# Evicting the output projection of a linear-attention layer from PSUM in two halves

## What is computed

```python
def ffn(x, weight):                       # binarised weights
    return jnp.einsum('bsi,oi->bso', x, jnp.sign(weight))
def attn(x, ...):                         # linear attention, 16 heads of 64
    Q = phi(x @ Wq.T + bq); K = phi(x @ Wk.T + bk); V = x @ Wv.T + bv   # phi = elu + 1
    KV = jnp.einsum('bhnd,bhne->bhde', K, V)
    out = jnp.einsum('bhnd,bhde->bhne', Q, KV)
    norm = jnp.einsum('bhnd,bhd->bhn', Q, K.sum(axis=2))[..., None] + 1e-6
    return (out / norm) @ Wo.T + bo
x = x + 0.5 * ffn(layernorm(x), w)        # y1, x is (32, 2048, 1024) f32
x = x + attn(layernorm(x), ...)           # y2
x = x + 0.5 * ffn(layernorm(x), w)        # y3, the output
```

## Time and profile before

| | |
|---|---|
| time before, median of 2 runs | 2089.19 us (2078.95 to 2099.43) |
| the profiled execution | 2094.45 us |
| its span on the slowest core, core 5 | 2092.9 us |
| spans of the 8 cores | 2068.7 to 2092.9 us |
| granted TensorE clock of the cores, mean | 0.982 to 0.995 |
| TensorE busy | 1783.9 us (85%) |
| ScalarE busy | 1236.2 us (59%) |
| VectorE busy | 778.9 us (37%) |
| first and last y2 eviction of pass 2 on core 5 | 1368.0 and 2076.3 us |

### The profile page before, as it was taken

How to read it: one execution, slowest core, us unless ns; L and a number is a source line. 1 busy time by engine, 2 the same in 40 slices (tenths; PEclk the granted TensorE clock), 3 DMA queues, 4 the chain that set the end, 5 groups by cost and what they waited for, 6 DMA issues and landing times.

```text
span 2092.9 us, 33187 instructions; the slowest of 8 cores (2068.7 to 2092.9 us)
## 1 busy us (share of the span) xinstructions
PE 1783.9 (85%) x10784; PEld 796.1 (38%) x10784; DVE 778.9 (37%) x2049; ACT 1236.2 (59%) x2025; POOL 147.5 (7%) x274
## 2 busy tenths in 40 slices
PE   0689999899899899988999989788888888888887
PEld 0233333333333333333333333344444444444443
DVE  2234333343343343333333333133443443443443
ACT  1476766767767767666776676544444444444443
POOL 1000000000000010000000000001011001011010
PEclk9999999999999999999999999989999999999999
DMA  8622222222222222222222222123333333333332
GB/s 186 120 88 87 69 87 66 88 90 66 87 90 66 88 92 92 89 65 87 77 79 89 68 88 68 46 101 113 115 126 115 112 126 106 122 126 111 117 126 76
DMA packets 134631, 199.35 MB, mean 95 GB/s; under 512 B 88384, under 2 KB 88384, under 8 KB 134464
## 3 DMA queue, kind: packets, MB, share of 16 engines
q0 software_dynamic: 32960, 109.08, 15.7%
q1 hardware_dynamic: 101504, 88.15, 13.7%
HBM read 104.87 MB, written 83.89 MB: 90 GB/s over the span
## 4 chain that ended last, share of the span: by engine, by line
PE 55%; ACT 25%; issue 11%; DVE 6%; DMA 3%; ACTq 1%; DVEq 0%; SPq 0%
PE pA L463 34%; PE pA L474 12%; DVE y2t L341 4%; PE pA L468 3%; ACT u1b L442 3%; ACT mnb L397 3%; ACT mxb L399 3%; ACT u2b L448 3%; PE pA L478 2%; ACT nb L357 2%; ACT kbQ L385 2%; ACT eb L398 2%; DMA stg<-wfT 2%; ACT kbQ L386 1%; ACT kbK L401 1%
## 5 line engine op out<-in xcount | busy, mean ns | idle before, releaser
L474 PE MATMUL pA<-wv,u1fm 128*128 128x512 bf16 x1024 | 258.2, 397 | 97.3 <-ACT kbK L401 97.3
L463 PE MATMUL pA<-sw,u2fm 128*128 128x512 bf16 x1024 | 234.6, 383 | 76.3 <-DVE y2t L341 75.1
L474 PE MATMUL pA<-wk,u1fm 128*128 128x512 bf16 x1024 | 242.4, 379 | 18.3 <-ACT kbQ L385 18.3
L442 ACT ACTIVATE u1b<-y2t 128x1024 bf16<-128x1024 f32 x64 | 67.7, 1057 | 300.5 <-DVE y2t L341 300.5
L463 PE MATMUL pA<-wo,attnfm 128*128 128x512 bf16 x1024 | 235.3, 383 | 5.2 <-DVE y3t L321 1.4
L463 PE MATMUL pA<-sw,u0fm 128*128 128x512 bf16 x1024 | 235.7, 384 | 0.0
L463 PE MATMUL pA<-wq,u1fm 128*128 128x512 bf16 x1024 | 232.1, 380 | 0.0
L474 PEld LDWEIGHTS pA<-wv,u1fm 128*128 128x128 bf16 x1024 | 93.4, 100 | 222.1 <-issue 137.8
L382 ACT ACTIVATE u2b<-y1t 128x1024 bf16<-128x1024 f32 x63 | 66.6, 1058 | 185.6 <-DVE y1t L287 185.6
L463 PEld LDWEIGHTS pA<-sw,u2fm 128*128 128x128 bf16 x1024 | 96.3, 98 | 194.5 <-issue 90.3
L287 DVE SCALAR_TENSOR_TENSOR y1t<-pA,xt 128x1024 f32<-128x1024 f32 x63 | 77.2, 1225 | 211.2 <-PE pA L463 211.2
(11 more groups left out here) (120 smaller groups left out, 2429.2 us busy)
## 6 DMA issues: line engine op xcount, KB each, us to landing
xt<-x SPq DMA_DIRECT2D x64, 512.0 KB, 3.8
y1scr<-y1t POOLq DMA_DIRECT2D x64, 512.0 KB, 3.8
y1in<-y1scr POOLq DMA_DIRECT2D x64, 512.0 KB, 4.5
out<-y3t SPq DMA_DIRECT2D x64, 512.0 KB, 2.6
qscr<-qfm POOLq DMA_DIRECT2D x64, 256.0 KB, 3.2
qfin<-qscr POOLq DMA_DIRECT2D x64, 256.0 KB, 4.7
qfm<-phiQ SPq DMA_TRANSPOSE x512, 2.3
stg<-wfT SPq DMA_DIRECT2D x4, 512.0 KB, 9.0
```

Source lines behind the costliest of these rows:

```text
L442: e.activation(u1b[:, 0, :], y2t[:, tw % 2, :], AF.Square, accum_out=sq3b[:, :]).then_inc(sSq3, 1)
L463: mm = e.matmul(dst[:, h*512:(h+1)*512], lhs_fm[:, c*P:(c+1)*P], w_sb[:, c, h*512:(h+1)*512], start=(c == 0), stop=(last and c == 7))
L474: mm = e.matmul(dst[:, h*512:(h+1)*512], lhs_fm[:, c*P:(c+1)*P], w_sb[:, c, h*512:(h+1)*512], start=(c == 0), stop=(last and c == 7))
```

## The change

The output projection wo is written with the halves outside: eight chunks and the bias of columns 0 to 511, an increment of `tWo`, then the same for columns 512 to 1023. VectorE takes y2 out of `pA2` in two instructions of 512 columns, each waiting for its half and each with a row sum of its own (`red3a`, `red3b`); a further 128x1 addition joins the two sums. `vY2` now counts two per tile, and its other users are adapted. FFN2 uses the `hw` form: its first half waits for the first half of y2 alone, its second half for the second. Two waits move: FFN2 now starts only when both halves of `u2fm` are there, and wo only when both halves of `attnfm` are there.

```diff
@@ gpsimd @@
-                e.wait_ge(vY2, t - 1)
+                e.wait_ge(vY2, 2 * (t - 1))
@@ vector @@
-                    v.wait_ge(tWo, t)
+                    v.wait_ge(tWo, 2 * t - 1)
                     v.wait_ge(dY1i[tw % 2], 16 * (tw // 2 + 1))
                     if t >= 3:
                         v.wait_ge(sU2, t - 2)
-                    v.scalar_tensor_tensor(y2t[:, tw % 2, :], pA2[:, :], 0.0, y1in[:, tw % 2, :],
+                    v.scalar_tensor_tensor(y2t[:, tw % 2, 0:512], pA2[:, 0:512], 0.0,
+                                           y1in[:, tw % 2, 0:512],
+                                           ALU.bypass, ALU.add, accum_out=red3a[:, :]).then_inc(vY2, 1)
+                    v.wait_ge(tWo, 2 * t)
+                    v.scalar_tensor_tensor(y2t[:, tw % 2, 512:1024], pA2[:, 512:1024], 0.0,
+                                           y1in[:, tw % 2, 512:1024],
                                            ALU.bypass, ALU.add, accum_out=red3b[:, :]).then_inc(vY2, 1)
+                    v.wait_ge(vY2, 2 * t)
+                    vsync(v, v.tensor_tensor(red3b[:, :], red3a[:, :], red3b[:, :], ALU.add))
                     v.wait_ge(sSq3, t)
@@ scalar @@
-                    e.wait_ge(vY2, t)
+                    e.wait_ge(vY2, 2 * t)
@@ tensor @@
                 if 3 <= t <= NT + 2:
-                    e.wait_ge(vY2, min(t - 1, NT))
+                    e.wait_ge(sU2fm, 2 * t - 4)
                     if t > NT:
                         e.wait_ge(vY3, t - 3)
                     proj(e, u2fm[:, (t - 3) % 2, :], sw, pA2[:, :], None, tFfn2,
-                         cw=(sU2fm, 2 * t - 5))
+                         hw=(vY2, min(2 * t - 3, 2 * NT - 1)))
@@ tensor, wo @@
                 if 1 <= t <= NT:
+                    e.wait_ge(sAttnfm, 2 * t)
                     if t >= 3:
                         e.wait_ge(vY3, t - 2)
-                    proj(e, attnfm[:, (t - 1) % 2, :], wo, pA2[:, :], bor, tWo,
-                         cw=(sAttnfm, 2 * t - 1))
+                    for h in range(2):
+                        for c in range(8):
+                            e.matmul(pA2[:, h*512:(h+1)*512], attnfm[:, (t - 1) % 2, c*P:(c+1)*P],
+                                     wo[:, c, h*512:(h+1)*512], start=(c == 0), stop=False)
+                        e.matmul(pA2[:, h*512:(h+1)*512], ones_row[0:1, :],
+                                 bor[0:1, h*512:(h+1)*512], start=False,
+                                 stop=True).then_inc(tWo, 1)
```

More of the change, by code:

```diff
@@ L97, in build_nc @@
         sq2b = sb("sq2b", [P, 1], F32)
+        red3a = sb("red3a", [P, 1], F32)
         red3b = sb("red3b", [P, 1], F32)
```

## The result

| | before | after |
|---|---|---|
| time, median | 2102.47 us (42 runs) | 2092.42 us (43 runs) |
| median without the disturbed executions | 2098.28 us (31 runs) | 2087.51 us (30 runs) |
| ratio of after to before | | 0.995, 95% interval 0.993 to 0.9969 |
| the profiled execution's span, slowest core (5) | 2092.9 us | 2097.3 us |
| span of core 4, clock 0.992 and 0.993 | 2070.1 us | 2062.0 us |

A forecast was written before the change was run, and what follows sets the result against it. No engine is full; a dependence loop through three engines bounds pass 2. Per tile -0.54 - 0.13 + 0.21 + 0.28 = -0.18 us, times 63 is -11, tail -0.7, together -12: 2089.19 to 2077 us, range 2060 to 2096 (8 in 10).

The forecast's parts named there:

- The level: Starting time of the kernel before, taken as 2089.19 us, the median of the runs shown; gives 2077 us.
- The period: Pass 2, y2 to y2: 11.14 us per tile before, forecast 10.96 after, -0.18 a tile.
- The path: Pass 2 loop through y2, statistics, `u2b`, transposes and wo, 11.14 us; FFN2 and its y2 stall claimed off it.
- The wait for all of attnfm: Start of wo: it must await the second `attnfm` copy, costing 0.28 us a tile on the loop (0.03 to 0.36).
- The new order of wo: wo half-major with two bias switches: 4.29 us instead of 4.08, costing 0.21 a tile on the loop.
- the gain of the split: y2 eviction: only the second half lies behind wo, gaining 0.54 us a tile; two fewer wait steps gain 0.13.
- Rival B: wo's start and second bias: costs exceed the shorter eviction, slower; +23 us, 2112, if a half costs a whole; chance 0.07.
- D: Whole change: halves gain what wo loses, no effect, 2089 us; chance 0.03 beyond the range.
- Rival A: TensorE's idle time before FFN2 is the limit: 75 us would go, 2014 us (-3.6%); chance 0.04.
- Rival C: TensorE clock falls to 1.2 GHz after stalls: 2113 us if every third tile has a slow FFN2; chance 0.04.
- the tail: End of pass 2: last FFN2 starts at about W+12.2 instead of W+12.9 (W is wo's start), -0.7 us.
- FFN2's early start: FFN2 starts right behind the `attn` transposes, 4.9 instead of 5.9 us after wo's start; its order and waits cost nothing.

The follow-up runs named there:

- the half wait: Changed kernel, but wo waits for the first half of `attnfm` before chunk 0 and the second before chunk 4: 10.45 us per tile, 2037.69 us against 2080.27.
- the bias first: Changed kernel with wo's two bias matmuls issued first, ahead of the wait for `attnfm`: 10.35 us per tile, ratio to before 0.9815.
- half FFN2: Changed kernel with only 4 of the 8 chunks of FFN2, result incomplete: 2143.68 us against 2080.27, period most often 12.55 us.
- the early copies: Changed kernel with ScalarE's two `attnfm` copies moved from behind `u2b` to behind the square of y2: 10.45 us per tile, 2034.26 us against 2080.39.
- bias first with early copies: Changed kernel with wo's bias matmuls issued first and the `attnfm` copies moved behind the square of y2: 10.35 us per tile, 2042.89 us.

## Why the prediction was right and where it was wrong

**The level, wrong.** The forecast of 2077 took 2089.19, the median of two runs, as the level of the kernel before. Over 42 runs its median is 2102.47, 13 us more (2098.28, 9 us more, by the second row of the table), and on the chips of the experiments it was 2078 to 2082. Of the 15 us by which 2077 misses 2092.42, 13 are this; the change itself was forecast at -12 us and measured at -10 to -11. Set against 2102.47, a time of 2077 would be a gain of 1.2%, more than twice the 0.5% that was measured. The step that failed is "from 2089.19 it is 2077": the change was forecast to 0.1% (0.994 for 0.995), the level was known to no better than 1%, and most of the range should have been spent on it.

**The period, right to 0.01 us.** 10.96 was forecast and measured, with 0.69 for a half, 4.29 for wo, 0.25 behind `attnfm` and 4.46 to the second half of y2. Two kernels with this period ran 12 and 15 us under the kernel before beside them (more work in FFN2, and FFN2 waiting for all of y2), one run each, where the forecast was 12. A half took 692 ns. That agrees with the 0.69 read off a slope between two rows, and with the 691 ns of the Trainium skill, *VectorE: DVE Perf Modes*, section "The TRN2 errata".

**The path, wrong in a way that the sum hid.** "So the y2 stall in front of FFN2 is off the loop" is the sentence that failed. In the kernel before FFN2 was on the longer of two loops, 11.14 against 10.92: adding 0.43 to it added 0.43 to the period, and taking 0.43 away brought only 0.22. The change is better told as three steps: the FFN2 loop falls away (-0.22), the `u2b` loop gets shorter by 0.54 + 0.13 - 0.21 (10.92 to 10.46, measured 10.45 with the half wait), and the late `attnfm` puts 0.51 on top. The sum, -0.18, is the same, because the forecast took wo's real start at 1712.23 as its zero and counted how much later it would start: an error in what held wo there cancels. It no longer cancels where one part is undone, as the half wait (10.45 for 10.68) and the bias first (10.35 for 10.49) showed. That the sum came out at 10.96 was in this part luck.

**The wait for all of attnfm: mis-sized.** 0.28 by the forecast, 0.51 by the run that undoes it. It is the costliest single line of the change: the changed kernel without it ran 42.6 us under the kernel before beside it, one run each.

**The new order of wo and the gain of the split: right.** The order cost 0.21 (4.29 for 4.08). Split and waits together gained the 0.67 by which the one-piece eviction is longer; no run parts the 0.54 from the 0.13. That this kernel took 11.63, as 11.14 + 0.21 + 0.28 said, is the same cancellation: by the two loops it is 10.92 + 0.21 + 0.51 = 11.64. Rival B had its mechanism right and its price too low to decide; D didn't occur.

**Rival A: rightly put low, for half a reason.** The stall of 75 us did close and the time did not follow. But its place was on the loop, and 0.22 x 63 = 14 us of it were real.

**Rival C: present at the margin.** In the tail the last FFN2 started at W+12.1, as forecast (12.2), but took 6.50 us, so that instead of -0.7 the tail gave +2.0 on core 5. The prediction had only its start in the sum, and left its length at 3.61 without a reason. "Such tiles should become rarer" rested on the sum of the gaps. It isn't borne out: between 1400 and 2000 us the clock falls to the lower level 6 times on the eight cores of before and 10 times on those of after. The runs have more of them where one gap is longer and TensorE has less to do (half FFN2), and five or six with the bias first, whose gap before the `u2b` transposes is 1.13. The half wait and the early copies, with a gap of 1.02, have none in that stretch.

**FFN2's early start:** its order and its half wait cost nothing, as forecast, and brought nothing (the run in which it waits for all of y2).

What stays open: why pass 1, with the same code, took 14 us longer on core 5 in the profiled execution of after than in that of before, and why four of its cores ran at 0.81 for 158 us. The clock was lower; what lowered it no run here tells. Nor is it shown why the level of the 42 runs lies 18 to 20 us above that of the experiments' chips.

## What to carry to other kernels

Write down every loop of dependences with its length, not only the one that the chain of waits shows: two that differ by 2% look like one, and a wait that ends under the tail of the instructions before it leaves no idle time in the profile. Where a wait is made coarser to suit a new order of matmuls (all of an operand instead of its first half), price it on its own; here that one line ate 0.51 of the 0.69 us a tile that the rest had won. And forecast the ratio from the trace, but the level from many runs.

## What the runs showed of the hardware that was not expected

Taking matmuls away made the kernel 3% slower: with gaps of 2.75 us in a period of about 12 us the granted clock was 0.85 over 250 us, against 1.00 with the gap of 1.03 in the tile of after shown above. A kernel with a period 0.10 us shorter ran 8.6 us longer (bias first with early copies against early copies alone, one run each); six of its tiles fell in part to the lower clock, which is worth 7 of the 8.6 us.

The granted clock also had a third value: 0.81, held for 158 us on cores 2 and 3 together, and at another time on cores 0 and 1 together, in one profiled execution. There a 512-column matmul of wo came every 0.26 us and not every 0.21.

A wait on TensorE costs 0.25 us from the releaser's end to the next matmul when it is reached early, and nothing that shows when it is already met while transposes are still running: 0.44 from the first of eight transposes to the next projection with two waits between, as against 0.66 when one of them was late.
